# State-space chunk: seven pieces of work one step sooner, direct term at TensorE's step 13

## What is computed

```
xi, z = split(x @ in_w.T)                       # 512 + 512 features
u     = silu(conv4(xi) + conv_b)                # causal, 4 taps
dt, B, C = split(u @ xproj_w.T)                 # 16 + 16 + 16
delta = softplus(dt @ dt_w.T + dt_b)
h_t   = exp(delta_t * A) * h_(t-1) + delta_t * B_t * u_t     # 512 x 16 states
y_t   = sum_n h_t[:, n] * C_t[n] + u_t * Dp     # the last term is the direct term
out   = (y * silu(z)) @ out_w.T
```

## Time and profile before

| | |
|---|---|
| median of 3 runs | 7189.09 us (7184.21 to 7191.36) |
| profiled execution | 7189.04 us, its span 7187.7 us |
| busy share | PE 80%, DVE 76%, POOL 62%, ACT 49% |
| granted TensorE clock, mean | 0.927 |
| scans L1204 | 1024 of 2277 ns |
| products L1866 | 1024 of 2360 ns |
| weighings L1214 | 856 of 1196 ns |
| exponentials L1716 | 4096 of 462 ns |
| state sums L1403 | 4096 of 621 ns |

### The profile page before, as it was taken

The page is one execution under the profiler, slowest core; times in us unless marked ns, Lnnn a source line. Parts: engine busy times, 40 slices in busy tenths (PEclk is TensorE's granted clock), DMA queues, the critical chain, the costliest instruction groups (busy, mean ns, idle before and its releaser), DMA issues. The chain is left out here.

```text
span 7187.7 us, 59936 instructions
## 1 busy us (share of the span) xinstructions
PE 5745.4 (80%) x18532; PEld 3299.7 (46%) x18532; DVE 5426.8 (76%) x6112; ACT 3531.9 (49%) x6962; POOL 4489.9 (62%) x2668
## 2 busy tenths in 40 slices
PE   5778788787787877878779787797877978778787
PEld 4444354443554435544455444554445544455444
DVE  5579954899648995489954998549986499765997
ACT  1177611775127751277512775127741377413774
POOL 3189840897419974199641996419954299543994
PEclk8899898999999998999989999899998999989999
DMA  2011110111101111011110111101111011110111
GB/s 87 17 37 44 37 47 17 41 43 47 36 21 38 43 49 37 15 40 43 46 37 15 40 43 47 44 7 43 43 46 42 11 43 42 43 42 12 46 43 41
DMA packets 238126, 271.70 MB, mean 38 GB/s; under 512 B 144906, under 2 KB 194994, under 8 KB 231860
## 3 DMA queue, kind: packets, MB, share of 16 engines
q1 hardware_dynamic: 237748, 267.25, 11.5%
HBM read 246.13 MB, written 21.07 MB: 37 GB/s over the span
## 5 line engine op out<-in xcount | busy, mean ns | idle before, releaser
L1866 POOL TENSOR_TENSOR wk<-wk 128x1024 f32<-128x1024 f32 x1024 | 2381.7, 2360 | 8.2
L1204 DVE TENSOR_TENSOR_SCAN wk<-ps,wk 128x1024 f32<-128x1024 f32 x1024 | 2317.8, 2277 | 91.2 <-ACT ps L1716 58.8
L1403 PE MATMUL ps<-wk,ident 128*128 128x512 f32 x4096 | 2028.8, 621 | 24.4 <-DVE wk L1224 24.4
L1716 ACT ACTIVATE ps<-wk,Aneg 128x255 f32<-128x255 f32 x4096 | 1704.1, 462 | 684.8 <-DVE wk L1204 674.7
L440 POOL TENSOR_SCALAR rstd<-mv 128x4 f32<-128x4 f32 x146 | 38.3, 263 | 1966.7 <-DVE mv L433 1966.7
L1403 PEld LDWEIGHTS ps<-wk,ident 128*128 128x128 f32 x4096 | 746.1, 200 | 647.2 <-issue 616.9
L1214 DVE TENSOR_TENSOR wk<-wk,ps 128x1024 f32<-128x1024 f32 x856 | 1024.1, 1196 | 11.8 <-DVE wk L1204 7.3
L546 POOL TENSOR_TENSOR wk<-wk 128x4096 f32<-128x4096 f32 x64 | 529.3, 8278 | 301.1 <-ACT wk L668 301.1
L1398 PE MATMUL ps<-wk,sel 112*128 112x256 bf16 x856 | 245.7, 287 | 588.1 <-DVE wk L1214 578.6
L1346 PE MATMUL ps<-xnp,inT 128*128 128x256 f32 (+1 forms) x2048 | 581.8, 411 | 160.4 <-ACT wk L1568 80.5
L1346 PEld LDWEIGHTS ps<-xnp,inT 128*128 128x128 f32 x2048 | 403.1, 203 | 469.8 <-ACT wk L1568 133.9
(11 more groups left out here) (198 smaller groups left out, 8016.5 us busy)
## 6 DMA issues: line engine op xcount, KB each, us to landing
wk<-bc_scr SPq DMA_DIRECT2D x256, 512.0 KB, 3.6
wk<-bc_scr SPq DMA_DIRECT2D x56, 384.0 KB, 3.4
wk<-in_wgT SPq DMA_DIRECT2D x8, 1536.0 KB, 6.5
wk<-in_wuT SPq DMA_DIRECT2D x8, 1536.0 KB, 9.6
wk<-in_wdn SPq DMA_DIRECT2D x8, 1536.0 KB, 6.4
wk<-in_x SPq DMA_DIRECT2D x18, 512.0 KB, 4.0
o_scr<-wk SPq DMA_DIRECT2D x64, 128.0 KB, 3.0
wk<-o_scr SPq DMA_DIRECT2D x32, 256.0 KB, 3.4
```

What stands on the lines that cost most here:

```text
L1204: V.tensor_tensor_scan(h, in_time(d, flat(decay(m))), h, 0.0, ALU.mult, ALU.add).then_inc(scanned, 1)
L1403: mm = nc.tensor.matmul(bank(j), ident[:], h[:, 2 * j:2 * j + 2, :] .rearrange("p e t -> p (e t)"), start=first, stop=last)
L1716: nc.scalar.activation(decay(m)[:, e, rest(d)], dl[g % 2][:, e, rest(d)], ACT.Exp, scale=Aneg[:, d, e, n:n + 1]).then_inc(dA_done, 1)
L1866: nc.gpsimd.tensor_tensor(hb[n], du[g % 2], col(Bb[j % 2][:, n % NB, :]) .broadcast_to([P, NDI, MC]), ALU.mult).then_inc(dbu, 1)
```

## The change

All tables of steps below move by one, except that of the gate Z, of XD and of `INJ`, which stay; the direct term goes from step 1 to step 13 on TensorE. No instruction is added or removed.

```diff
-            PRE_PE = {0: (XD, 0), 2: (LG, 0), 3: (LG, 1), 8: (X, 0), 9: (X, 1), 10: (X, 2),
-                      11: (X, 3), 12: (Z, 0), 13: (Z, 1), 14: (Z, 2), 15: (Z, 3)}
-            Z_ACT, XD_ACT, LG_ACT = {0: 0, 1: 1, 2: 2, 3: 3}, 4, {6: 0, 7: 1}
-            OUT_PE, OUT_DVE = {4: (0, 0), 5: (0, 1), 6: (1, 0), 7: (1, 1)}, 9
+            PRE_PE = {0: (XD, 0), 1: (LG, 0), 2: (LG, 1), 7: (X, 0), 8: (X, 1), 9: (X, 2),
+                      10: (X, 3), 12: (Z, 0), 13: (Z, 1), 14: (Z, 2), 15: (Z, 3)}
+            Z_ACT, XD_ACT, LG_ACT = {0: 0, 1: 1, 2: 2, 3: 3}, 4, {5: 0, 6: 1}
+            OUT_PE, OUT_DVE = {3: (0, 0), 4: (0, 1), 5: (1, 0), 6: (1, 1)}, 8
...
-            XE_PE = {4: (0, 0), 5: (1, 0), 6: (0, 1), 7: (1, 1)}
-            XE_ACT = {8: (0, 0), 9: (1, 0), 10: (0, 1), 11: (1, 1)}
+            XE_PE = {3: (0, 0), 4: (1, 0), 5: (0, 1), 6: (1, 1)}
+            XE_ACT = {7: (0, 0), 8: (1, 0), 9: (0, 1), 10: (1, 1)}
...
-            CONV = {10: 0, 11: 1, 12: 2, 13: 3}
-            TAP = {11: 0, 12: 1, 13: 2, 14: 3}
+            CONV = {9: 0, 10: 1, 11: 2, 12: 3}
+            TAP = {10: 0, 11: 1, 12: 2, 13: 3}
...
-            SOFT = {8: "abs", 9: "exp", 10: "ln", 11: "relu"}
-            SILU, INJ, DIRECT = 15, 13, 1
+            SOFT = {7: "abs", 8: "exp", 9: "ln", 10: "relu"}
+            SILU, INJ, DIRECT = 14, 13, 13
```

## The result

The changed kernel takes 7217.58 us (median of 6 runs, 7206.78 to 7224.65) against 7189.30 us for the kernel before beside it: a ratio of 1.0038, 95% interval 1.0027 to 1.0049. It is slower by 28 us, and slower than the range of 7168 to 7208 that was given. Its profiled execution took 7223.39 us with a span of 7222.1, 34.4 us longer than that of before.

The account below looks back on a forecast made before the run. VectorE was taken to bound the stage, with two or three idle microseconds per unit to win. From 7189.04 us, −11.6 − 7.8 + 2.4 + 14.4 = −2.6 gave 7186.5 us, range 7168 to 7208.

Parts of the forecast that it names:

- ScalarE's chain, units 1 to 5: First convolution 16.24 us behind scan 6: 0.79 us won in 23 units, 0.39 lost in 17, 11.6 net gain.
- clock fall between second and third X: TensorE idle around the second X, so its clock falls: 0.36 us in each of 40 units, 14.4 us lost.
- units 6 and 7, evictions: Eviction waits of 0.28 and 0.69 us go as the direct term leaves their way: 7.8 us won at most.
- units 6 and 7, direct term at step 13: In unit 7 it lands near the stage's end: 0.3 us per sequence on the path, 2.4 us lost.
- unit 0: No short steps or output parts; its chain only shifts, hidden behind the same wait for the tap: cost nothing.
- 23 slow and 17 other units: Units 1 to 5 by kind, from 38.5 us of eviction waits: first convolution 20.34 or 19.16 us behind scan 6.
- the low clock holds: Rival, chance 0.12: low clock from second through third X; 7208 us in half of 40 units, 7244 in all.
- two points of decision: Third convolution's mean wait per unit that tests the low-clock rival: 0.43 us no gain, 0.8 slower by over 0.2%.
- No convolution is there to absorb a wait.: Said of units 6 and 7, as the ground for evictions' waits there counting as time: 7.8 us won at most.
- 1.8 us of direct term: Eight matmuls on TensorE ahead of the evictions of units 6 and 7; moving them should end the waits there.
- the direct term in the way of the C row: Rival, chance 0.04: at step 13 it costs 1.2 us in each of 56 units, 67 us on top, 7254 us.
- GpSimd's carried state: Sign of a wrong forecast: a first scan waits for it; GpSimd's lead was to shrink from 3.6 to 2.1 us.

Follow-up runs that it names:

- e5_direct_behind_x: The changed kernel with the direct term issued behind the second X piece, at TensorE's step 8 in place of 13: 7193.44 us, ratio 1.0000.
- e4_soft_unit6: The changed kernel with the softplus of unit 6 alone back at its old steps 8 to 11: 7197.62 us, ratio 1.0015.
- e2_shift_only: The changed kernel with the direct term back at step 1, so the shift alone: 7216.21 us, ratio 1.0040.
- e6_both: The changed kernel with second and third pooled sums one step sooner and unit 6's softplus at its old steps: 7168.75 us, ratio 0.9975.
- e1_direct_only: The kernel before with the direct term alone moved, from step 1 to step 13: 7231.66 us, ratio 1.0061.
- e8_all: The changed kernel with the direct term behind the second X, unit 6's softplus at its old steps and "abs" at step 6: 7159.43 us, ratio 0.9961.

## Why the prediction was wrong

Forecast and measured, for the profiled execution and by the terms of the sum:

```
term                                          forecast   measured
ScalarE's chain, units 1 to 5                    -11.6      -11.0
clock fall between second and third X            +14.4      +25.0
units 6 and 7, evictions                          -7.8
units 6 and 7, direct term at step 13             +2.4     +17.2 in all
unit 0                                             0        +5.7
work ahead of and between the stages               0        -2.5
```

*ScalarE's chain* was right, in its mechanism and its size. Units 1 to 5 became 14.0 us longer, of which the third convolution's wait is 25.0; without it they gain 11.0. In e5_direct_behind_x, where that wait is gone, they are 12.9 us shorter than before. The first convolution begins 16.18 to 16.28 us behind scan 6 in all 40 units (forecast 16.24). A unit that had taken 60.26 us and has no wait at the third convolution takes 59.42 now, 0.84 less (forecast 0.79), and one of 59.08 became 0.34 longer (forecast 0.39). The count of 23 slow and 17 other units, taken from one total, is that of the trace: 23 of the 40 took 60.2 us or more.

*The clock fall* was placed right and sized wrong. This is the first of the three steps that failed: "A fall costs 1.7 us on that path if it lies wholly on it", less 1.0 us of spare time, and then a middle of 0.36 us a unit. The 1.7 us came from a fall in the output parts, where the clock was back with the next state sum. Here it was still at 0.50 under the third X in 15 units, and the state sum and X, 2.8 us of work in the prediction's own figures, took 5.4 (2414.59 to 2419.95). The time lost is then not 0.7 us in a unit but 1.5. That was the rival "the low clock holds", held for unlikely since the rows of before showed no such case; 26 of 40 third convolutions waited, 25.0 us in sum, 0.63 each of the 40, which lies between that rival's two points of decision (0.43 and 0.8). It was named with the reason for it, two idle stretches in a row, and given 0.12. The upper end of the prediction's own term, 28 us, came nearer to the sum of 25.0 than the middle taken, but by the wrong division: it has 0.7 us in every unit, and 14 of the 40 waited for nothing, while 15 waited about twice the 0.7. (The Trainium skill, "TensorE: Matmul & The Clock Gate", section "What's actually happening", has it that activity releases the throttle. This case's traces agree: with 1.89 us of matmuls more in that place the clock stayed at 1.00 in e5_direct_behind_x.)

*Unit 6* is the second step that failed, and the larger one for the sign: "No convolution is there to absorb a wait." The sentence was right and was applied to evictions only. The convolution in units 1 to 5 was the step that took up ScalarE's block of "ln" and two table loads; the prediction followed that block in these five units and in unit 0, and in unit 6 it didn't look for the cover. Two lines of the trace of before would have told: the end of the exponentials behind the block, and the layer-norm work that stood in front of the scan in that same step. The eviction's 0.28 us went as forecast; 1.85 us came, eight times. e4_soft_unit6 took it away alone. (The Trainium skill, "ScalarE: Activation LUTs", section "What ACT_TABLE_LOAD costs", gives about 1283 ns for a load and 1380 ns more for a drain. The trace has the 1.28 us, and the next activation begins 1.30 us behind the load's start: the second part doesn't show here.)

*Unit 7* was to lose its eviction's wait of 0.69 us. It waits 1.31 in the third sequence, and the unit is 4.5 us longer in sum:

```profile
2665.70 0.69 DVE L1230 TENSOR_TENSOR ytok<-ps,ytok 128x512 f32<-128x512 f32 x1 [1.31 <-PE ps L1369]
```

The way ahead of the output parts was free of the direct term, as forecast, but the direct term was not what the eviction had waited for. TensorE stood for 6.74 us ahead of the C row at 2657.70 and did what follows at a clock of 0.50 (2655.80 to 2662.40). The same idle stretch was there in before, and longer, with the direct term at step 1 (fifth sequence, that of the earlier trace rows):

```profile
4416.09 0.39 PE L1398 MATMUL ps<-wk,sel 112*128 112x256 bf16 x1 [8.38 <-DVE wk L1214]
```

Nor does the term's place decide. With the shift and the term at step 1 (e2_shift_only) four of the eight evictions wait 1.30 to 1.43 us and four 0.40 to 0.47; with both moved, in e6_both, they wait 0.54 to 0.64; with the term alone moved (e1_direct_only) 0.64, and unit 7 is 1.9 us shorter than before. What goes with the wait, in all the traces with the shift, is how late the clock comes back: 0.33 to 0.47 us of wait where it is back 6.1 to 6.4 us behind scan 6, 1.28 to 1.51 where it is back at 8.0 to 9.5. So the third step that failed is that the "1.8 us of direct term" were what stood in the eviction's way: its wait goes with the clock. Why that comes back later in after than in e6_both stays open. The direct term's tail at step 13 was sized right: the last weighing of the stage waits 5.4 us in sum and waited 3.5 before, 1.9 against 2.4.

*Unit 0* was costed at nothing and lost 5.7 us: its first convolution begins 18.6 or 19.05 us behind scan 6, where a mere shift of 3.31 from 21.8 gives 18.5. A fall now begins 14.7 to 16.8 us behind scan 6, where it began at 20.2 in seven of eight sequences. The late start is there with the shift alone: e2_shift_only, with the direct term back at step 1, has 19.05 us in four sequences and 18.52 in four. Another 2.4 of the 5.7 us are the weighings of unit 0's last state, which wait in unit 1's first step for the C row behind the direct term.

*Outside the stage* nothing was forecast. It gave 2.5 us back here, and 19 to 20 us in the traces of e5_direct_behind_x, e6_both and e8_all. By that measure the stage of e8_all is 27.5 us shorter than before and the profiled execution, at 7142.49, is a lucky one of its five.

Of the other rivals, the direct term in the way of the C row was seen at 2.4 us in sum (0.18 to 0.42 us, eight times) and not at 1.2 us a unit, though it grew to 10.1 us in e6_both; GpSimd's carried state didn't end a wait that it hadn't ended before.

## What to carry to other kernels

Before a block of work is moved by a step, list for every kind of iteration what covers it at its new place, and start with the iterations that leave out a part of the body: the cover may be that part. Work that is ready at any time and stands in an idle stretch of TensorE isn't time to be saved; before it is moved, read the granted clock ahead of and behind it, and if it has to move, move it into the longest idle stretch that the change makes. And cost a fall of the clock by all the work that stands between its start and the wait that ends, at twice its time, not by the mildest fall of the trace before.

## What the runs showed of the hardware

The clock fell after idle stretches of 1.29 and 2.17 us with a matmul group of 1.14 us between them (unit 3 of after). What a fall cost went with when it began, over all 40 units of that trace: 1.35 to 1.49 us of wait for VectorE where it began 19.4 to 20.2 us behind scan 6, 0.13 to 0.52 where it began at 20.3 to 22.2. With 1.89 us of matmuls more in front of it an X piece ended 2.6 us sooner behind scan 6 (unit 3 of e5_direct_behind_x and of after). And work that the edits don't touch took 393 us in some sequences and up to 398 in others of one execution; in 13 traces its length goes with the time at the low clock in it, 393 to 394 us with 66 us of it and 397 to 398 with 76. Over eight sequences that is as large as the effect under study.
